# Attention and soft mixture of experts on one core: front and first block scheduled by pairs of tiles, dispatch from a hyperbolic tangent

## The chip, the cores and the metric

One core of one Trainium2 chip runs the whole program. The metric is the device time in microseconds (us) from launch to end, as the median of several runs. The kernel is written in Bass: every engine has its own list of instructions, written out by hand, and the lists meet at semaphores. Short names: PE is TensorE, PEld its weight load, DVE VectorE, ACT ScalarE, POOL GpSimd, SP SyncE (here a queue for DMAs).

## The reference

```python
def ln(x): return (x - mean(x)) / sqrt(var(x) + 1e-5)
# x: (2, 2048, 256); C = 256; N = 64 experts, P = 32 slots each

def attn(x):                       # linear attention, no softmax
    h = ln(x) * norm_w + norm_b
    q, k, v = split(h @ qkv_w.T + qkv_b)
    o = ((q @ k.T) / sqrt(C)) @ v
    return x + o @ proj_w.T + proj_b

def ffn(x):
    logits   = einsum('bmd,dnp->bmnp', x, phi)
    dispatch = softmax(logits, axis=0)            # over the batch, 2 entries
    combine  = softmax(logits over all n*p)       # over 2048 slots
    slots = einsum('bmd,bmnp->bnpd', x, dispatch)
    y     = einsum('bnpd,nde->bnpe', slots, W) + b
    return einsum('bnpd,bmnp->bmd', y, combine)

x = x + ln(attn(ln(x)))
x = x + ln(ffn(ln(x)))
```

## The kernel before, in words

A tile is 128 tokens; each of the two batch entries has 16 (`NJ`). Five stages follow one another.

*Front* (to 51 us). Tiles of x are loaded in groups of four (`load_x`), DVE takes mean and variance (`stats`), POOL works out the scales (`x_terms`), ACT normalises (`xhat`), PE adds each tile to a 256x256 sum and transposes it (`s_tile`, L1184 and L1193). Attention is linear, so it becomes one matrix A for each batch entry: `weight_products` (L1171, L1175) multiplies prepared weights, `T_step`, `R_step`, `A_step` (L1200, L1210, L1220, L1222) combine them with the sum. The prepared weights come from DVE (`bias_columns` L871 to L877, `primed_weights` L891, L894) and from one product on POOL (L430). `phi`, the slot matrix, is split on DVE into two fp16 halves (L927, L929) after a maximum over all partitions on POOL (L437).

*Second norm*. For each pair of tiles PE multiplies with A (`h_pair`, L1234). DVE adds x (`add_x`, L945), ACT squares (`y_squares`, L643), POOL takes the power -1/2 (`y_terms`), DVE adds to the residual (`residual`, L962) and takes statistics (`stats_x2`, L972 and L975), POOL takes the next power (`x3_terms`), ACT writes the normalised x3 (`x3_float`, L652) and its fp16 high half (`x3_hi`), POOL its low half (`x3_lo`, L471). All of it in groups of four tiles, `GROUPS_Y` and `GROUPS_X`.

*Dispatch and slots*. A softmax over two entries is a sigmoid of the difference of logits. POOL subtracts the two batch entries (`xd_diff`, L480), ACT and POOL split the difference (`xd_hi`; `xd_lo`, L487), SP transposes it by DMA (L314) and, for later, x3 (L317). Four blocks of 512 slots follow, each over 16 tiles: PE multiplies the difference with a block of phi (`d_tile`, L1266, six matmuls), ACT takes two sigmoids (`dispatch`, L700) and copies the logit difference, which is stored to DRAM; DVE splits both sigmoids into fp16 halves of 1024 columns (`split`, L952 and L954); PE multiplies tile and dispatch into the slots (`slots`, L1278, twelve matmuls). After a block DVE takes the slots out of PSUM (`slots_out`, L1027). Block 0 is unrolled and interleaved with the second norm, whose late groups it must wait for; blocks 1 to 3 are loops (`block_pe` and so on), in which PE also does the experts of the block before (`y_product`, L1291), with the bias added by DVE (`y_bias`, L1036, L1039). The last group has its `y_product` after block 3, against the loads of expert weights.

*Combine* (from 414 us to the end). For each tile logits again, exp on ACT (L774), transposes by DMA, three products with y (L1351, L1352, L1355), the last norm and the store.

What sets the order is therefore the written list of each engine. This is the part of PE's list in block 0:

```python
for j in range(NJ):
    if j % GJ == 0:
        pe.wait_ge(x3l_ready, 2 * (j // GJ + 1))
    slots(0, j)
    if j + 2 < NJ:
        d_first(j + 2)
    else:
        d_tile(1, j + 2 - NJ)
    if j in (2, 3):
        h_pair(12 + j)
```

## Time and profile before

| what | us |
|---|---|
| median of 3 runs (lowest, highest) | 691.34 (690.93, 692.81) |
| the profiled execution, its own time | 690.47 |
| its span, first to last instruction | 688.7 |
| busy: PE, DVE, ACT, POOL | 618.7, 440.0, 348.2, 246.7 |
| share of the span: PE, DVE, ACT, POOL | 90%, 64%, 51%, 36% |
| PE's mean granted clock, share of 2.4 GHz | 0.97 |

The profile is of one execution. Its span is shorter than its time by what lies around the program. A time of day in the text, as "at 95.72", is counted from the start of the span. A PE row of the timeline gives the stretch from the first start to the last end of its matmuls, and matmuls overlap: the next starts while the last drains.

### The profile page before, as it was taken

How to read it: one execution, taken by the hardware profiler on the slowest of the kernel's cores; microseconds unless marked ns; L12 is line 12 of the kernel's file. 1: busy time of each engine (PE TensorE's matmuls, PEld its weight loads, DVE VectorE, ACT ScalarE, POOL GpSimd, SP SyncE). 2: the span in 40 equal slices, each digit the busy share in tenths (PEclk: the TensorE clock that was granted, in tenths of full speed). 3: DMA queues.
4: the chain of work that ended last, by engine and by line, in shares of the span. 5: the costliest groups of instructions: out<-in, count | busy, mean ns of one | idle time of the engine just before them, and what ended most of it. 6: DMA issues, size and time to landing. Idle time of an engine off the chain costs nothing.

```text
span 688.7 us, 12544 instructions
## 1 busy us (share of the span) xinstructions
PE 618.7 (90%) x3962; PEld 377.5 (55%) x3962; DVE 440.0 (64%) x795; ACT 348.2 (51%) x600; POOL 246.7 (36%) x510
## 2 busy tenths in 40 slices
PE   5899766887999999999999977799999999999992
PEld 4788522333444444444444434367777777777782
DVE  5937666845645555554655568877777777777750
ACT  4565585555433333444443328555566666655550
POOL 5632755954000000000000000166666555666666
PEclk9999969799999999999999999899999999999997
DMA  8900123225133343333334366499999899999991
GB/s 288 393 27 0 31 62 91 63 75 123 61 131 131 130 130 129 127 121 125 127 117 136 118 223 160 118 214 225 213 220 216 198 213 233 225 219 221 214 182 41
DMA packets 190238, 104.52 MB, mean 152 GB/s; under 512 B 152833, under 2 KB 178690, under 8 KB 187906
## 3 DMA queue, kind: packets, MB, share of 16 engines
q1 hardware_dynamic: 183408, 82.07, 48.1%
q10 hardware_dynamic: 6802, 22.09, 9.8%
q8 instruction: 16, 0.26, 0.2%
q14 instruction: 12, 0.10, 0.1%
HBM read 43.32 MB, written 23.07 MB: 96 GB/s over the span
## 4 chain that ended last, share of the span: by engine, by line
PE 66%; DVE 8%; POOL 8%; ACT 7%; issue 5%; DMA 3%; SPq 2%; POOLq 0%; DVEq 0%; ACTq 0%
PE psL L1278 19%; PE psL L1337 10%; PE bk L1266 9%; PE bk L1351 6%; PE bk L1355 6%; PE bk L1352 6%; PE bk L1291 4%; POOL small L395 2%; ACT r_y L652 2%; PE psL L1184 2%; POOL r_xn L471 2%; DMA r_xn<-in_proj_wT 1%; ACT xbuf L643 1%; DVE r L954 1%; ACT r L700 1%
## 5 line engine op out<-in xcount | busy, mean ns | idle before, releaser
L1278 PE MATMUL psL<-r,r_xn 128*128 128x512 f16 x768 | 183.0, 389 | 25.8 <-DVE r L954 25.5
L700 ACT ACTIVATE r<-bk,small 128x512 f32<-128x512 f32 x128 | 80.8, 682 | 140.5 <-PE bk L1266 139.5
L1278 PEld LDWEIGHTS psL<-r,r_xn 128*128 128x128 f16 x768 | 73.9, 100 | 126.8 <-DVE r L954 25.4
L1351 PE MATMUL bk<-r_xn,r 128*128 128x256 f16 x512 | 113.9, 273 | 7.0 <-DMA r<-r 4.0
L1352 PE MATMUL bk<-r_xn,r 128*128 128x256 f16 x512 | 113.8, 273 | 0.0
L952 DVE TENSOR_SCALAR r<-r 128x1024 f16<-128x1024 f32 x64 | 48.5, 758 | 89.8 <-ACT r L700 89.8
L1266 PE MATMUL bk<-phs,xx 128*128 128x512 f16 (+1 forms) x384 | 95.0, 385 | 4.5 <-DMA xx<-r 4.5
L1337 PE MATMUL psL<-phs,xx 128*128 128x512 f16 x384 | 88.3, 387 | 5.7 <-DVE small L1059 4.9
L534 POOL PARTITION_ALL_REDUCE small<-small x1 | 1.2, 1233 | 253.3 <-DVE small L1130 253.3
L774 ACT ACTIVATE r<-psL,small 128x1024 f32<-128x1024 f32 x32 | 38.2, 1198 | 87.7 <-DVE small L1059 87.7
L954 DVE SCALAR_TENSOR_TENSOR r<-r 128x1024 f16<-128x1024 f32 x64 | 80.2, 1253 | 2.2
L1266 PEld LDWEIGHTS bk<-phs,xx 128*128 128x128 f16 x384 | 38.0, 99 | 52.0 <-issue 8.5
L1337 PEld LDWEIGHTS psL<-phs,xx 128*128 (+1 forms) x384 | 37.8, 99 | 51.0 <-issue 11.0
L1355 PE MATMUL bk<-r_xn,r 128*128 128x256 f16 x512 | 61.1, 273 | 0.1
L1351 PEld LDWEIGHTS bk<-r_xn,r 128*128 128x128 f16 x512 | 50.0, 98 | 17.0 <-DVE r_xn L1115 3.7
L587 ACT ACTIVATE r<-bk 128x512 f32<-128x512 f32 (+2 forms) x97 | 50.3, 519 | 16.4 <-PE bk L1355 11.7
L1063 DVE CUSTOM_DVE_ANT_0 r<-psL,xx 128x512 f32<-128x512 f32 x64 | 40.4, 687 | 24.1 <-ACT r L774 24.1
L1352 PEld LDWEIGHTS bk<-r_xn,r 128*128 128x128 f16 x512 | 50.1, 98 | 7.1
L395 POOL TENSOR_TENSOR small<-small,epst 128x1 f32<-128x1 f32 (+2 forms) x58 | 52.0, 897 | 4.8
L1355 PEld LDWEIGHTS bk<-r_xn,r 128*128 128x128 f16 x512 | 50.0, 98 | 6.1 <-DMA r<-xx 0.4
L1075 DVE TENSOR_REDUCE small<-psL 128x1 f32<-128x512 f32 x64 | 41.2, 685 | 11.1 <-PE psL L1337 10.7
L1052 DVE TENSOR_TENSOR xx<-r,xx 128x1024 f16<-128x1024 f32 x32 | 37.9, 1222 | 11.4 <-ACT xx L587 11.4
(117 smaller groups left out, 811.8 us busy)
## 6 DMA issues: line engine op xcount, KB each, us to landing
r<-in_ffn_w SPq DMA_DIRECT2D x16, 1024.0 KB, 6.6
xx<-logit_difference ACTq DMA_DIRECT2D x15, 1024.0 KB, 5.4
logit_difference<-r SPq DMA_DIRECT2D x48, 256.0 KB, 2.4
xres<-in_x SPq DMA_DIRECT2D x8, 512.0 KB, 9.0
logit_difference<-r ACTq DMA_DIRECT2D x16, 256.0 KB, 2.4
out<-r SPq DMA_DIRECT2D x32, 128.0 KB, 2.4
expert_bias<-r ACTq DMA_DIRECT2D x1, 2048.0 KB, 26.3
r<-in_phi SPq DMA_DIRECT2D x1, 2048.0 KB, 18.7
```

The lines of the kernel that those rows point to most:

```text
L395: return nc.gpsimd.tensor_tensor(o, v, epst[:, 0:1].broadcast_to([P, n]), ALU.pow)
L587: return nc.scalar.activation(o, i, ACT.Copy, scale=scale)
L700: ins = nc.scalar.activation(sF[:, j % 2, s, :], bk[j % 2][:, :], ACT.Sigmoid, scale=kap[:, s:s + 1])
L952: own.add(V.tensor_scalar(shl[:, j % 2, 0], sF[:, j % 2], S_SCALE, None, ALU.mult))
L954: V.scalar_tensor_tensor(shl[:, j % 2, 1], sF[:, j % 2], S_SCALE, shl[:, j % 2, 0], ALU.mult, ALU.subtract).then_inc(s_split, 1)
L1075: own.add(V.tensor_reduce(m4[:, kb:kb + 1], psL[:, 512 * kb:512 * kb + 512], AX_X, ALU.max))
L1266: ins = mm(bk[j % 2][:, :], xxT[:, 1, j, hx, k, :], phs[:, hp, k, bass.ds(nb * 512, 512)], start=(k == 0 and hx + hp == 0), stop=(k == K - ...
L1278: ins = mm(psL[:, i * 512:(i + 1) * 512], x3n[:, b, j, hx, k * P:(k + 1) * P], shl[:, j % 2, hs, b, :], start=(j == 0 and hx + hs == 0), s ...
L1337: ins = mm(psL[:, kb * 512:(kb + 1) * 512], xxT[:, 0, bass.ds(j, 1), hx, k, :].rearrange("p j t -> p (j t)"), phs[:, hp, k, kb * 512:(kb + ...
L1351: mm(acc, eT[b][:, 0, t, :], yhl[:, b, t, 0, :], start=(t == 0), stop=False)
L1352: mm(acc, eT[b][:, 0, t, :], yhl[:, b, t, 1, :], start=False, stop=False)
L1355: ins = mm(acc, eT[b][:, 1, t, :], yhl[:, b, t, 0, :], start=False, stop=(t == NT - 1))
```

## The change

- The front loads the first four tiles in two groups. DVE, no longer POOL, multiplies the weights with the norm weight; the centring of the projection goes behind `primed_weights` and has a signal of its own; `weight_products` goes from before tile 14 to after tile 17. The all-reduce of phi goes ahead of the second `residual_terms`.
- The second norm goes by pairs of tiles instead of fours: twice the number of power instructions on POOL, of half the columns.
- The batch difference and its low half go from POOL to DVE.
- The dispatch of entry 0 is (1 + t)/2 and that of entry 1 is (1 - t)/2 with t = tanh(d/2). ACT takes one tanh for two sigmoids, DVE splits 512 columns instead of 1024, and the slots matmuls of both entries read the same t. The constant half of each token sum is put in by `slots_out`, from sums that PE makes once (`token_sums`, `half_sums`) and ACT copies.
- The stores of the logit difference in block 0 go from ACT's queue to SP's, between the transposes.
- The lists of all engines for the second norm and block 0 are written anew; loops and stages behind are otherwise the same.

```diff
-        GROUPS_Y = [0, 1, 4, 5, 2, 6, 3, 7]
-        GROUPS_X = [0, 4, 1, 5, 2, 6, 3, 7]
+        X_GROUPS = [(0, 0, 2), (0, 2, 2)] + [(b, j, GJ) for b in range(B) for j in range(0, NJ, GJ) if b + j]
+        Y_ORDER = [(0, 0), (0, 1), (0, 2), (0, 3), (1, 0), (1, 1), (1, 2), (0, 4), (1, 3), (0, 5), (1, 4), (0, 6), (1, 5), (0, 7), (1, 6), (1, 7)]
+        X_ORDER = [(0, 0), (1, 0), (0, 1), (1, 1), (0, 2), (1, 2), (0, 3), (1, 3), (0, 4), (1, 4), (0, 5), (1, 5), (0, 6), (1, 6), (0, 7), (1, 7)]
...
 # SP
+            def store_d(nb, j):
+                sp.wait_ge(d_copied, nb * NJ + (j + 3))
+                sp.dma_start(d_dram[j, :, bass.ds(nb * 512, 512)], dS[:, j % 2, :]).then_inc(d_stored[j % 2], 16)
+            turn_xd(0); turn_xd(1); store_d(0, 0); store_d(0, 1); turn_xd(2); store_d(0, 2)
+            store_d(0, 3); turn_xd(3); store_d(0, 4); store_d(0, 5); turn_x1(0); turn_xd(4)
...
 # POOL
-                if g == NG - 1:
-                    pool.wait_ge(par_loaded, 16 * N_PAR)
-                    nc.gpsimd.tensor_tensor(w_aug, w_raw, wbc.unsqueeze(1).broadcast_to([P, KS, C]),
-                                            ALU.mult).then_inc(waug_ready, 1)
...
+            residual_terms(0)
             pool.wait_ge(gmax_in, 1)
             nc.gpsimd.partition_all_reduce(gm[:, 0:1], pm[:, 0:1], P, bass.bass_isa.ReduceOp.max).then_inc(gmax_out, 1)
+            residual_terms(1)
...
+            y_terms(0, 0); y_terms(0, 1); x3_terms(0, 0); y_terms(0, 2); x3_lo(0, 0); y_terms(0, 3)
+            y_terms(1, 0); y_terms(1, 1); x3_terms(1, 0); x3_terms(0, 1); x3_terms(1, 1); x3_lo(1, 0)
...
 # ACT
-                for s in range(B):
-                    ins = nc.scalar.activation(sF[:, j % 2, s, :], bk[j % 2][:, :], ACT.Sigmoid, scale=kap[:, s:s + 1])
-                ins.then_inc(s_ready, 1)
+            def tanh(nb, j):
+                act.wait_ge(d_done, nb * NJ + (j + 1))
+                act.wait_ge(s_split, nb * NJ + (j + 1))
+                nc.scalar.activation(tF[:, j % 2, :], bk[j % 2][:, :], ACT.Tanh, scale=khalf).then_inc(t_ready, 1)
+            def d_copy(nb, j):
+                act.wait_ge(d_stored[j % 2], nb * (8 * NJ) + (16 * (j // 2) + 16))
+                copy(dS[:, j % 2, :], bk[j % 2][:, :]).then_inc(d_copied, 1)
+            def token_sums_copy():
+                act.wait_ge(xs_done, 1)
+                for b in range(B):
+                    copy(xsum[:, b], bk[2 + b][:, :]).then_inc(xs_copied, 1)
...
+            xd_hi(7); x3_hi(1, 7); d_copy(0, 12); tanh(0, 13); d_copy(0, 13); token_sums_copy()
+            tanh(0, 14); d_copy(0, 14); tanh(0, 15); d_copy(0, 15); half_sums_copy()
...
 # DVE
+            def weight_scale():
+                dve.wait_ge(par_loaded, 16 * N_PAR)
+                own.add(V.tensor_tensor(w_aug, w_raw, wbc.unsqueeze(1).broadcast_to([P, KS, C]), ALU.mult))
...
             stats(3)
+            stats(4)
             proj_bias()
+            weight_scale()
+            stats(5)
             bias_columns()
-            stats(4)
             primed_weights()
-            stats(5)
+            centre_projection()
             stats(6)
             stats(7)
+            stats(8)
...
-                own.add(V.tensor_scalar(shl[:, j % 2, 0], sF[:, j % 2], S_SCALE, None, ALU.mult))
+                own.add(V.tensor_scalar(thl[:, j % 2, 0], tF[:, j % 2], S_SCALE, None, ALU.mult))
                 own.wait()
-                V.scalar_tensor_tensor(shl[:, j % 2, 1], sF[:, j % 2], S_SCALE, shl[:, j % 2, 0],
+                V.scalar_tensor_tensor(thl[:, j % 2, 1], tF[:, j % 2], S_SCALE, thl[:, j % 2, 0],
                                        ALU.mult, ALU.subtract).then_inc(s_split, 1)
...
+            def xd_diff(p):
+                t2, o2 = slice(2 * p, 2 * p + 2), slice(2 * (p % 2), 2 * (p % 2) + 2)
+                dve.wait_ge(x3_ready, max(X_AT[0, p], X_AT[1, p]) + 1)
+                if p >= 2:
+                    dve.wait_ge(xdl_ready, p - 1)
+                V.tensor_tensor(xd[:, o2], xy[:, 0, t2, :], xy[:, 1, t2, :], ALU.subtract).then_inc(xd_ready, 1)
+            def xd_lo(p):
+                o2 = slice(2 * (p % 2), 2 * (p % 2) + 2)
+                dve.wait_ge(xdh_ready, p + 1)
+                V.tensor_tensor(xdn[:, o2, 1, :], xd[:, o2], xdn[:, o2, 0, :], ALU.subtract).then_inc(xdl_ready, 1)
...
-                                        1.0 / (X_SCALE * S_SCALE), None, ALU.mult).then_inc(slots_evac, 1)
+                                        (0.5 - b) / (X_SCALE * S_SCALE), xhalf[:, i:i + 1],
+                                        ALU.mult, ALU.add).then_inc(slots_evac, 1)
...
 # PE
             for t in range(B * NJ):
-                if t == 14:
-                    weight_products()
                 s_tile(t)
                 if t == NJ + 1:
+                    weight_products()
                     T_step(0)
...
-                                     shl[:, j % 2, hs, b, :], start=(j == 0 and hx + hs == 0), stop=(j == NJ - 1 and hx == 1))
+                                     thl[:, j % 2, hs, :], start=(j == 0 and hx + hs == 0), stop=(j == NJ - 1 and hx == 1))
...
+            def token_sums():
+                pe.wait_ge(y_added, B * NJ)
+                pe.wait_ge(x3l_ready, B * NJ // 2)
+                for b in range(B):
+                    for r in range(NJ // GJ):
+                        for g in range(GJ):
+                            ins = mm(bk[2 + b][g * Q:(g + 1) * Q, :], ones16[:, :],
+                                     x3n[:, b, r * GJ + g].rearrange("p h c -> p (h c)"), start=(r == 0), stop=(r == NJ // GJ - 1))
+                ins.then_inc(xs_done, 1)
+            def half_sums():
+                pe.wait_ge(xs_copied, B)
+                for k in range(K):
+                    for b in range(B):
+                        for h in range(2):
+                            ins = mm(bk[2][:, k * B + b:k * B + b + 1], xsum[:, b, h * C + k * P:h * C + (k + 1) * P], half_mean,
+                                     start=(h == 0), stop=(h == 1))
+                ins.then_inc(xhalf_done, 1)
+            d_first(0); d_first(1); h_pair(0, 7); slots_first(0); d_first(2); slots_first(1)
+            d_first(3); slots_first(2); h_pair(1, 6); d_first(4); slots_first(3); d_first(5)
...
+            d_first(14); token_sums(); slots_first(13); d_first(15); slots_first(14); d_tile(1, 0)
+            half_sums(); slots_first(15); d_tile(1, 1)
```

PE in the front, after the transposes of tile 13; L1184 and L1193 are a tile of the sum, L1171 and L1175 the weight products. Before:

```order
L1193 MATMUL bk<-ident,xbuf 128x128 x2
L1171 MATMUL bk<-r_xn 128x256 x4
L1175 MATMUL bk<-r_xn 128x256 x4
L1184 MATMUL psL<-xbuf 128x256
L1184 MATMUL psL<-xbuf 128x128
```

Now, after tile 17 (L1129 and L1138 are a tile, L1114 and L1120 the weight products, L1145 the T step):

```order
L1138 MATMUL bk<-ident,xbuf 128x128 x2
L1114 MATMUL bk<-r_xn 128x256 x4
L1120 MATMUL bk<-r_xn 128x256 x4
L1145 MATMUL psL<-ident,r_xn 128x128
L1129 MATMUL psL<-xbuf 128x256
L1129 MATMUL psL<-xbuf 128x128
```

The products stand four tiles later, right ahead of the first step that needs them.

DVE at the first splits of block 0. Before, L952 and L954 are the split, L962 the residual, L972 and L975 the statistics, four tiles at once:

```order
L952 TENSOR_SCALAR r<-r 128x1024
L954 SCALAR_TENSOR_TENSOR r<-r 128x1024
L962 SCALAR_TENSOR_TENSOR xres<-r_y,small,xres 128x256 x4
L952 TENSOR_SCALAR r<-r 128x1024
L954 SCALAR_TENSOR_TENSOR r<-r 128x1024
L972 BN_STATS stat<-xres 128x6 x4
L975 BN_AGGR small<-stat 128x2 x4
```

Now, in the third split of the block (L898 and L900 the split, L891 the add of x, L929 the batch difference, L935 its low half):

```order
L891 SCALAR_TENSOR_TENSOR r_y<-xres,small,bk 128x256 x2
L929 TENSOR_TENSOR r<-r_y 128x512
L898 TENSOR_SCALAR r<-r 128x512
L900 SCALAR_TENSOR_TENSOR r<-r 128x512
L935 TENSOR_TENSOR r<-r 128x2x256
L907 SCALAR_TENSOR_TENSOR xres<-r_y,small,xres 128x256 x2
L917 BN_STATS stat<-xres 128x6 x2
L920 BN_AGGR small<-stat 128x2 x2
L898 TENSOR_SCALAR r<-r 128x512
```

Between two splits stand pieces of two tiles, and the difference and its low half stand around a split.

SP's queue after the loads. Before, the loads (L304, L307) and then only the transposes of block 0 (L314 of the difference, L317 of x3):

```order
L304 DMA r<-in_ffn_w 128x8x256 x2
L307 DMA r<-expert_bias 128x256 x2
L314 DMA_TRANSPOSE xx<-r 128x8x128 x2
L317 DMA_TRANSPOSE xx<-r_xn 128x16x128
L314 DMA_TRANSPOSE xx<-r 128x8x128 x2
```

Now (L320 the difference, L326 x3, L331 the stores of the logit difference):

```order
L320 DMA_TRANSPOSE xx<-r 128x8x128 x2
L331 DMA logit_difference<-r 128x512 x2
L320 DMA_TRANSPOSE xx<-r 128x8x128
L331 DMA logit_difference<-r 128x512 x2
L320 DMA_TRANSPOSE xx<-r 128x8x128
L331 DMA logit_difference<-r 128x512 x2
L326 DMA_TRANSPOSE xx<-r_xn 128x16x128
```

Two stores stand between one transposed pair and the next.

## Rows read from the trace of the kernel before

**Rows 1.** Windows by stage: us, then busy time and instructions of PE, PEld, DVE, ACT, POOL; clock, DMA

```profile
9.60:51.46 41.86, 39.21 (x228) 35.18 (x229) 27.59 (x75) 26.61 (x54) 22.94 (x37) 0.96 0.64 228
51.46:84.69 33.23, 28.72 (x133) 24.43 (x132) 22.23 (x58) 19.68 (x58) 16.32 (x22) 0.99 0.07 14
84.69:186.90 102.21, 77.85 (x316) 33.67 (x316) 65.67 (x108) 57.65 (x113) 53.13 (x52) 0.89 0.32 81
186.90:394.40 207.50, 206.10 (x1224) 91.43 (x1224) 111.86 (x129) 82.30 (x141) 0.00 (x0) 1.00 0.38 124
```

**Rows 2.** Groups of PE, 51.46 to 186.9: busy, mean ns | idle before and its releaser

```profile
L1278 PE MATMUL psL<-r,r_xn 128*128 128x512 f16 x192 | 50.6, 420 | 24.3 <-DVE r L954 24.3
L1266 PE MATMUL bk<-phs,xx 128*128 128x512 f16 x108 | 27.9, 399 | 4.5 <-DMA xx<-r 4.5
```

**Rows 3.** Timeline of PE: start us, length us, what, count [idle before, releaser]

```profile
84.69 4.16 PE L1266 MATMUL bk<-phs,xx 128*128 128x512 f16 x12 [4.51 <-DMA xx<-r]
95.72 5.28 PE L1278 MATMUL psL<-r,r_xn 128*128 128x512 f16 x12 [6.86 <-DVE r L954]
...
133.23 5.30 PE L1278 MATMUL psL<-r,r_xn 128*128 128x512 f16 x12 [3.36 <-DVE r L954]
...
163.37 2.76 PE L1278 MATMUL psL<-r,r_xn 128*128 128x512 f16 x12 [1.69 <-DVE r L954]
...
394.45 2.76 PE L1278 MATMUL psL<-r,r_xn 128*128 128x512 f16 x12 [0.95 <-DVE r L954]
...
412.69 1.93 PE L1291 MATMUL bk<-r 128*32 128x256 f32 x32 [2.53 <-DMA r<-in_ffn_w]
```

**Rows 4.** Timeline of PE in the front

```profile
6.69 1.11 PE L1162 MATMUL bk<-ident,bT 128*64 128x128 f32 x4 [6.69 <-DMA bT<-in_ffn_bT]
...
18.11 0.82 PE L1184 MATMUL psL<-xbuf 128*128 128x256 f32 x4
...
22.48 0.82 PE L1184 MATMUL psL<-xbuf 128*128 128x256 f32 x4
...
26.11 3.68 PE L1171 MATMUL bk<-r_xn 128*128 128x256 f32 x8 [2.60 <-DVE r_xn L894]
29.63 1.89 PE L1175 MATMUL bk<-r_xn 128*128 128x256 f32 x8
```

**Rows 5.** Timeline of DVE: first add, and the first split of block 0

```profile
54.25 1.84 DVE L945 SCALAR_TENSOR_TENSOR r_y<-xres,small,bk 128x256 f32<-128x256 f32 x4
...
93.51 0.69 DVE L952 TENSOR_SCALAR r<-r 128x1024 f16<-128x1024 f32 x1 [3.04 <-ACT r L700]
94.24 1.23 DVE L954 SCALAR_TENSOR_TENSOR r<-r 128x1024 f16<-128x1024 f32 x1
```

**Rows 6.** Timeline of POOL in the front

```profile
15.61 3.68 POOL L430 TENSOR_TENSOR r_xn<-r_xn 128x1536 f32<-128x1536 f32 x1 [1.28 <-DMA r_xn<-in_proj_wT]
...
46.16 0.38 POOL L437 PARTITION_ALL_REDUCE small<-small  x1 [5.55 <-issue]
```

**Rows 7.** Groups of the whole program, PE's y product and ACT's dispatch

```profile
L700 ACT ACTIVATE r<-bk,small 128x512 f32<-128x512 f32 x128 | 80.8, 682 | 140.5 <-PE bk L1266 139.5 <-ACT r L587 0.9
...
L1291 PE MATMUL bk<-r 128*32 128x256 f32 x512 | 30.9, 382 | 3.4 <-DMA r<-in_ffn_w 3.4
```

**Rows 8.** Timeline of ACT at the first exp

```profile
408.83 1.28 ACT L774 ACT_TABLE_LOAD   x1 [18.10 <-DVE small L1059]
```

**Rows 9.** Groups of POOL, 51.46 to 186.9

```profile
L487 POOL TENSOR_TENSOR r<-r 128x512 f16<-128x512 f32 x8 | 11.5, 1458 | 2.2 <-ACT r L587 2.2
L480 POOL TENSOR_TENSOR r<-r_y 128x512 f32<-128x512 f32 x8 | 10.2, 1296 | 7.2 <-ACT r_y L652 7.2
```

**Rows 10.** Instructions of line 314, the transposes of the difference on SP

```profile
DMA to landing us min/median/max: 3.1/3.2/4.8
```

**Rows 11.** Groups of DVE, 84 to 187

```profile
L954 DVE SCALAR_TENSOR_TENSOR r<-r 128x1024 f16<-128x1024 f32 x17 | 22.6, 1332 | 0.6
L952 DVE TENSOR_SCALAR r<-r 128x1024 f16<-128x1024 f32 x17 | 16.1, 947 | 31.9 <-ACT r L700 31.9
```

466 lines of the change are left out of this document (179 added, 287 removed).

## The prediction

> **What bounds the kernel now.** I read the windows by stage first, then the groups of TensorE inside the stage with most idle time, then TensorE's own timeline, and last the engines that end its waits. The windows [rows 1] are to be read as length of the stage against PE's busy time. From 186.90 to 394.40 us, blocks 1 to 3, PE is busy 206.10 of 207.50 us at clock 1.00: what only relieves another engine can gain nothing there. The idle time that the change addresses lies ahead of it: 2.7 us in the front (41.86 less 39.21) and 28.9 us from 51.46 to 186.90 (4.51 and 24.36), and in the last of these stretches the granted clock is .89.
>
> Who ends the waits: before the slots matmuls (L1278) PE waits 24.3 us in all for DVE's L954, the second half of the split, and before L1266 4.5 us for the first transposed difference [rows 2]. In the timeline [rows 3] the gaps are 4.51, 6.86 and 3.36 us at 84.69, 95.72 and 133.23. Behind the last two, twelve matmuls take 5.28 and 5.30 us instead of 2.76: PE has fallen from 2.4 to 1.2 GHz, so an idle stretch is paid twice. L954 is only the last link. Groups of four tiles pass through add, square, power, residual, statistics, power, normalise, difference, split in two halves and transpose, and each hop holds back four tiles at once.
>
> **The front.** The weight products stand after tile 13. There PE waits 2.60 us for the DVE chain and then needs 3.68 us for eight matmuls of which the next eight take 1.89 [rows 4]. They now stand after tile 17. A tile costs .874 us (five from 18.11 to 22.48), so PE arrives 3.5 us later than it does now, at 27.0 instead of 23.5. The DVE chain is led now by the product with the norm weight, 1536 columns, which on POOL took 3.68 us [rows 6]; on DVE 1024 columns with two inputs take 1.23 [rows 5], so about 1.9. It was done at 26.1 before; with the centring moved behind it and one statistics group moved ahead I take 25 to 27. So the wait goes: 2.60 us. Without a gap the low clock goes too: 3.68 - 1.89 = 1.79. The first x load is halved, but ACT's first work hangs on the bias rows, for which PE waits until 6.69 [rows 4]; I take 0. The front gives **-4.4 us**, bounds 0 (DVE's chain late by as much as now) and -5. PE begins the h products at 47.1 instead of 51.46.
>
> DVE must by then have split phi. It waits for POOL's all-reduce at 46.16 and adds from 54.25 [rows 5, 6], 8.1 us behind. The all-reduce now goes ahead of the second residual group; with the earlier statistics I put it at 41, and DVE's first add at 49.1, when the first h pair is there. If the all-reduce stayed at 46, PE would run ahead by its banks, but all pairs would come 5 us later: +5 as a bound.
>
> **Block 0.** From 51.46 to 186.92 PE takes 135.5 us. Its own work at full clock: 192 slots and 108 difference matmuls at .216 (twelve end 2.76 after the first starts, .38 of it drain; [rows 3] at 163.37), 64.8 us. 32 h tiles of four fp32 matmuls, also .216 (the 1.89 for eight, [rows 4]), 27.7; the second batch's R and A are eight such matmuls each, 3.5, with a transpose and two bias matmuls 4.2. Sum 96.7. The other 38.8 us are 28.9 idle and 9.9 low clock and drains.
>
> New work on PE: 32 matmuls for the token sums, 512 columns into 32 rows, in turn into four row groups. L1291 has that form in fp32, where 256 columns cost the .216 that 512 cost in fp16: 32 of them take 1.93 us [rows 3], though the mean of one is .382 [rows 7]. So four run side by side and the 32 here cost 1.9 (bound: one after another, 6.9). For sixteen fp32 matmuls of one column there is no row; between .06 each, the pace of L1291, and .216: .9 to 3.5, I take 2.4, nearer to the second, since each brings fp32 weights of 128 columns. **PE's work is then 101.0 us, and without idle time block 0 ends at 47.1 + 101.0 = 148.1.** Blocks 1 to 3 keep their twelve slots matmuls for a tile.
>
> Can the others feed it? Sums of the two windows [rows 1]: DVE 87.9 now; 17 splits lose half of .69 + 1.23 [rows 5] (-16.3); eight differences and eight low halves of 512 columns come in at half of 1.23 (+9.9): 81.5. ACT 77.3, less 17 times one of two sigmoids (.68, [rows 7]): 65.7, and its 16 stores go to SP. POOL 69.4 less 10.2 + 11.5 [rows 9] is 47.7; its terms are twice as many instructions of half the size, and even if all of it doubled it would be 95. None reaches 101; DVE is the fullest. What remains is the loop from pair to pair: difference 1.3, tanh .7, split .96, low half .6, transpose .4 to start and 3.2 to land [rows 10], next difference. With five hand-overs of .1 that is 7.7, and PE takes 2 x 3.9 = 7.8 for two tiles: no slack. The order gives it some later (the low half stands two or three tiles ahead). But DVE's splits average 1.33 and .95 in this stretch against the 1.23 and .69 of the single rows [rows 11, 5]. I add 1 to 1.3 us for each of seven pairs: **8 us of idle time**. Bounds: 0, and 24.3, what PE waits for L954 now. In it is SP: difference tiles' stores now stand between the transposes, so that a transpose can wait for a copy that ACT has yet to make.
>
> Block 0 ends at 148.1 + 8 = 156.1 instead of 186.9: **-30.8**, of which the 4.4 of the front are a part.
>
> **Behind it.** Blocks 1 to 3: 0, hidden by PE's 206 us; without that cover the halved splits would gain, not lose. At 394.45 PE waits .95 for L954 behind a bias add [rows 3]; half of that split goes, so **-0.9**. Of the table loads the one before exp (1.28 at 408.83, [rows 8]) goes if tanh and exp need none between them. It is hidden: at 412.69 PE waits for expert weights [rows 3], not for exp. 0.
>
> Sum -30.8 - .9 = **-31.7**. The profiled execution took 690.47 (span 688.7), .87 below the median of the runs, 691.34: 658.8 by its clock, **659.6** as median.
>
> **Rivals.**
> 1. *PE never waits.* For it: every other sum is below PE's. Against: the loop without slack. 691.34 - 38.8 - .9 = 651.6. Chance 0.13.
> 2. *DVE and POOL hold each other up.* The differences leave POOL for DVE, and each has two SBUF inputs. The splits' two halves take 2.28 us here instead of 1.92 [rows 11, 5], a fifth on top. If the rest of DVE's 81.5 grow alike, to 97, DVE is as full as PE and no split is early: 1.3 us late at each of 16 tiles makes 21 us of waits instead of 8: 659.6 + 13 = 673. 0.13. The Trainium skill, "SBUF — State Buffer", section "Who interferes with whom", says that a VectorE instruction with two SBUF inputs and a GpSimd instruction that reads SBUF shut each other out for a whole instruction. The long splits agree with it; by that rule what moves from GpSimd to VectorE doesn't end the contention, it leaves fewer large GpSimd instructions to contend with.
> 3. *The clock stays low (slower).* Place: difference and slots matmuls of block 0. PE would idle a little before each tile instead of much before each fourth, and restart at 1.2 GHz each time, as behind the gap at 95.72. Price: 300 matmuls at .43 instead of .216, +64.8 on 659.6: 724. It makes the kernel slower once 31.7/64.8 = 49% of them run low. Against: behind the gaps PE is back at 2.76 for a group one tile later. 0.03.
> 4. *The change does not do what it says*: pairs in a fixed order wait on each other as fours did and block 0 keeps its length. Only front and .9 count: 686. 0.03.
>
> **Numbers.** Forecast (3 to 15 us of idle time in block 0) 0.68; the rivals 0.13, 0.13, 0.03, 0.03. Range 650.5 to 673: it takes in rival 1, rival 2 up to its value, and the bounds of the token sums (+5), of the front (+4.4) and of DVE's start (+5). About 0.3% (2 us) is what a measurement of this kernel can tell from no change. Faster 0.96, same 0.01, slower 0.03.
>
> **What would show it.** Right: the weight products run without a wait, eight in 1.9; h products from 47; first difference tile near 74 instead of 84.69; no gap over 2 us before a slots group; clock at 1.00 up to block 1, whose slots begin near 156; 501 us from there to the end. Wrong: a gap of PE at the token sums or half sums (it would wait for ACT's copies), transposes landing after more than 5 us, or PE busy for more than 101 us between the h products and block 1.

## The result and the profile after

The changed kernel takes **660.06 us** (median of 4 runs, 658.74 to 666.30) against 691.35 for the kernel before in the same measurement (690.93 to 692.81): a ratio of 0.956, 95% interval 0.951 to 0.961. Forecast were 659.6 us and a range of 650.5 to 673. The profiled execution took 660.40 us with a span of 658.4. The total is right to .5 us; the terms are less so, and several errors cancel. Of all executions behind this document one is left out, of the run called "first group of four" below, which took 1086.52 us at a granted clock of .56.

| us | before | forecast | after |
|---|---|---|---|
| PE's first h product | 51.46 | 47.1 | 48.76 |
| DVE's first add | 54.25 | 49.1 | 53.88 |
| first difference tile on PE | 84.69 | near 74 | 77.47 |
| slots of block 1 begin | 186.92 | 156.1 | 159.83 |
| from there to block 3's last slots group | 207.53 | 206.6 | 205.26 |
| from there to the last y product | 18.24 | as before | 17.27 |
| from there to the end of the span | 276.0 | as before | 276.0 |

The windows of the profile after, at the bounds that the forecast gave the stages, a little ahead of the measured ones (columns as in [rows 1]):

```profile
9.60:47.00 37.40, 36.43 (x215) 32.90 (x216) 26.36 (x78) 26.61 (x53) 15.04 (x32) 1.00 0.72 260
47.00:76.00 29.00, 27.88 (x133) 23.79 (x132) 21.75 (x50) 15.86 (x45) 18.70 (x34) 1.00 0.02 5
76.00:156.50 80.50, 73.08 (x363) 34.80 (x362) 58.15 (x128) 51.62 (x119) 50.27 (x83) 1.00 0.44 104
156.50:364.00 207.50, 207.50 (x1238) 93.75 (x1236) 76.07 (x131) 56.27 (x96) 0.00 (x0) 1.00 0.38 124
```

The stretch from the first difference tile to block 1 has lost 24.36 - 7.42 = 17 us of idle time (between its measured bounds, 77.47 and 159.83, 7.10 are left), and the granted clock is 1.00 in it instead of .89. The timeline of PE after, the rows with the waits that answer to [rows 3], the new work, and the two places behind the blocks:

```profile
57.06 1.99 PE L1165 MATMUL psL<-r_xn 128*128 128x256 f32 x8 [1.12 <-ACT r_xn L554]
77.47 2.75 PE L1202 MATMUL bk<-phs,xx 128*128 128x512 f16 x12 [0.32 <-DMA xx<-r]
100.68 2.75 PE L1214 MATMUL psL<-r,r_xn 128*128 128x512 f16 x12 [1.34 <-DVE r L900]
109.52 2.75 PE L1214 MATMUL psL<-r,r_xn 128*128 128x512 f16 x12 [0.91 <-DVE r L900]
118.59 1.46 PE L1202 MATMUL bk<-phs,xx 128*128 128x512 f16 x6 [0.94 <-ACT r L554]
131.13 2.75 PE L1214 MATMUL psL<-r,r_xn 128*128 128x512 f16 x12 [1.48 <-DVE r L900]
143.22 1.47 PE L1202 MATMUL bk<-phs,xx 128*128 128x512 f16 x6 [0.84 <-DMA xx<-r]
144.62 1.91 PE L1252 MATMUL bk<-r_xn,ones 128*32 128x512 f16 x32
154.25 1.84 PE L1262 MATMUL bk<-small,xbuf 128*128 128x1 f32 x16
365.09 2.76 PE L1214 MATMUL psL<-r,r_xn 128*128 128x512 f16 x12 [0.15 <-DVE r L900]
382.36 1.93 PE L1227 MATMUL bk<-r 128*32 128x256 f32 x32 [1.70 <-DMA r<-in_ffn_w]
```

From the first h product on no gap is longer than 1.48 us up to block 1, and no group of twelve takes more than 2.76: PE never falls to 1.2 GHz in block 0. For the experiments one row says most: the window from PE's first h product to its first slots of block 1, "block 0" from here on. For the changed kernel it is:

```profile
48.76:159.83 111.07, 102.52 (x497) 58.40 (x496) 80.36 (x181) 67.91 (x163) 68.97 (x117) 1.00 0.33 79
```

PE is busy 102.52 us and idle 8.55 (forecast: 101.0 and 8). More than 101 us of work in this stretch was one of the forecast's signs of being wrong, the only one that came; its cause is below. For the kernel before the same window, 51.46 to 186.92, has 106.58 busy and 28.9 idle.

### The profile page after: what moved, and what is told of

Read it like the earlier page. It is cut to its first block, busy times and chain, and to the rows that moved or that the text cites. A ratio compares the mean times of both kernels' runs of the same rounds, so it can differ in the third digit from the quotient of the medians.

```text
span 658.4 us, 12694 instructions
## 1 busy us (share of the span) xinstructions
PE 613.0 (93%) x4010; PEld 378.4 (57%) x4010; DVE 396.6 (60%) x813; ACT 310.7 (47%) x545; POOL 239.4 (36%) x555
## 4 chain that ended last, share of the span: by engine, by line
PE 67%; POOL 9%; DVE 8%; issue 7%; DMA 5%; ACT 3%; SPq 1%; POOLq 0%; DVEq 0%; ACTq 0%
PE psL L1214 20%; PE psL L1296 11%; PE bk L1202 10%; PE bk L1310 7%; PE bk L1311 7%; PE bk L1314 7%; PE bk L1227 4%; POOL small L415 4%; DMA r_xn<-in_proj_wT 1%; DMA r<-r 1%; DVE xres L907 1%; DMA xx<-r 1%; POOL r_xn L486 1%; DVE r_xn L1058 1%; DMA r<-in_ffn_w 1%
## 5 line engine op out<-in xcount | busy, mean ns | idle before, releaser
L1214 PE MATMUL psL<-r,r_xn 128*128 128x512 f16 x768 | 176.3, 379 | 4.7 <-DVE r L900 4.7
L639 ACT ACTIVATE r<-bk,small 128x512 f32<-128x512 f32 x64 | 43.8, 685 | 151.8 <-PE bk L1202 150.7
L1202 PE MATMUL bk<-phs,xx 128*128 128x512 f16 (+1 forms) x384 | 93.2, 379 | 2.8 <-DMA xx<-r 1.9
L898 DVE TENSOR_SCALAR r<-r 128x512 f16<-128x512 f32 x64 | 28.1, 439 | 88.9 <-ACT r L639 88.9
L415 POOL TENSOR_TENSOR small<-small,epst 128x2 f32<-128x2 f32 (+3 forms) x75 | 57.5, 767 | 6.2
L1018 DVE TENSOR_REDUCE small<-psL 128x1 f32<-128x512 f32 x64 | 41.2, 686 | 10.6 <-PE psL L1296 10.3
L900 DVE SCALAR_TENSOR_TENSOR r<-r 128x512 f16<-128x512 f32 x64 | 44.3, 693 | 2.2
```

The lines of the kernel that those rows point to most:

```text
L415: return nc.gpsimd.tensor_tensor(o, v, epst[:, 0:1].broadcast_to([P, n]), ALU.pow)
L639: nc.scalar.activation(tF[:, j % 2, :], bk[j % 2][:, :], ACT.Tanh, scale=khalf).then_inc(t_ready, 1)
L900: V.scalar_tensor_tensor(thl[:, j % 2, 1], tF[:, j % 2], S_SCALE, thl[:, j % 2, 0], ALU.mult, ALU.subtract).then_inc(s_split, 1)
L1018: own.add(V.tensor_reduce(m4[:, kb:kb + 1], psL[:, 512 * kb:512 * kb + 512], AX_X, ALU.max))
L1202: ins = mm(bk[j % 2][:, :], xxT[:, 1, j, hx, k, :], phs[:, hp, k, bass.ds(nb * 512, 512)], start=(k == 0 and hx + hp == 0), stop=(k == K - ...
L1214: ins = mm(psL[:, i * 512:(i + 1) * 512], x3n[:, b, j, hx, k * P:(k + 1) * P], thl[:, j % 2, hs, :], start=(j == 0 and hx + hs == 0), stop ...
```

## Experiments

The runs came in four groups, and in each the kernel before was run too: 690.85, 691.82, 690.33 and 690.05 us. Each ratio is to that. Times of different groups are compared below as they stand, so differences of 1 to 2 us between them are not told apart.

| run | us | ratio, 95% interval | block 0 | PE idle in it |
|---|---|---|---|---|
| the changed kernel | 660.06 | 0.951 to 0.961 | 111.07 | 8.55 |
| pairs, two sigmoids | 674.06 | 0.974 to 0.978 | 121.95 | 19.48 |
| fours, tanh | 683.33 | 0.988 to 0.993 | 129.49 | 19.28 |
| differences on POOL | 675.33 | 0.977 to 0.982 | 126.67 | 21.70 |
| adds by batch | 658.73 | 0.952 to 0.956 | 110.87 | 8.79 |
| weight products at 14 | 662.93 | 0.955 to 0.960 | 115.36 | 9.56 |
| no sums | 657.31 | 0.948 to 0.953 | 107.19 | 8.32 |
| stores on ACT | 665.81 | 0.959 to 0.966 | 114.05 | 10.08 |
| first group of four | 660.05 | 0.953 to 0.958 | 110.83 | 8.24 |
| POOL also adds | 674.97 | 0.974 to 0.980 | 125.29 | 19.35 |
| POOL also fills | 670.44 | 0.968 to 0.973 | 121.55 | 16.97 |
| lists shifted | 659.38 | 0.951 to 0.956 | 108.61 | 6.74 |
| lists again | 658.57 | 0.953 to 0.955 | 107.70 | 5.82 |

### Pairs without tanh, tanh without pairs

The first undoes the tanh in the changed kernel (dispatch, splits, token sums):

```diff
-                nc.scalar.activation(tF[:, j % 2, :], bk[j % 2][:, :], ACT.Tanh, scale=khalf).then_inc(t_ready, 1)
+                for s in range(B):
+                    ins = nc.scalar.activation(sF[:, j % 2, s, :], bk[j % 2][:, :], ACT.Sigmoid, scale=kap[:, s:s + 1])
+                ins.then_inc(t_ready, 1)
...
-            d_first(14); token_sums(); slots_first(13)
+            d_first(14); slots_first(13)
```

> The changed kernel with its new lists, but with two sigmoids and splits of 1024 columns as before; token sums and half sums, no longer needed, are left out. Theory A (order by pairs carries the gain, the tanh only gives the loop its slack): the loop of a pair grows by half a split, .96 us, and one activation, .6 us, so 1.6 us x 8 pairs = +13, less 3.5 us of sums: 668 to 672 us. Theory B (the tanh carries the gain, since DVE and ACT lose 16 and 11 us of work): most of the 31 us comes back, 683 us or more. Blocks 1 to 3 get back 1.5 to 2.3 us under both.

The second puts the same tanh, splits and sums into the kernel before and leaves its order of fours:

```diff
+                if j == 12:
+                    token_sums()
+                if j == 14:
+                    half_sums()
```

> The kernel before with its groups of four and its old lists, but with one tanh, splits of 512 columns, token sums and half sums. Theory A: the nine waits before slots stay, each shorter by some .96 + .6 us where split or sigmoid ended it, about -10 in block 0 and -2 in blocks 1 to 3, plus 3.5 of sums: 681 to 687 us. Theory B: 670 us or less.

Measured: 674.06 and 683.33. The first is 2 us above the range of its theory A and far below theory B, the second is inside theory A. The first run has all other edits too (front, differences on DVE, stores on SP); the second has tanh and sums alone. Against 690.85 pairs alone bring 16.8 us and tanh alone 7.5, 24.3 in all; together they bring 31.3 (691.35 - 660.06), 7 more than the sum. By the profiled executions, against 690.47, it is 5. PE's timelines say where from, first of the pairs without tanh, then of the fours with it:

```profile
108.14 4.08 PE L1213 MATMUL psL<-r,r_xn 128*128 128x512 f16 x12 [2.80 <-DVE r L902]
...
144.40 4.44 PE L1213 MATMUL psL<-r,r_xn 128*128 128x512 f16 x12 [3.73 <-DVE r L902]
```

```profile
84.06 5.28 PE L1290 MATMUL bk<-phs,xx 128*128 128x512 f16 x12 [5.00 <-DMA xx<-r]
92.41 4.44 PE L1302 MATMUL psL<-r,r_xn 128*128 128x512 f16 x12 [3.08 <-DVE r L975]
113.23 4.40 PE L1302 MATMUL psL<-r,r_xn 128*128 128x512 f16 x12 [4.24 <-DVE r L975]
138.61 5.30 PE L1302 MATMUL psL<-r,r_xn 128*128 128x512 f16 x12 [3.99 <-DVE r L975]
```

In each alone PE still idles 19 us in block 0, against 28.9 before and 8.55 with both, and some of its gaps are still long enough that the groups behind them take 4.08 to 5.30 us instead of 2.75. PE's loss beyond its own work (96.7 us, with the sums 100.4) was 38.8; it is 25.3 with pairs, 29.0 with tanh, 10.6 with both. Idle time nearly adds up: 9.4 and 9.6 us less alone, 20.3 together. The rest of the loss, low clock and drains, doesn't: 9.9 us before, 5.8 with pairs, 9.8 with tanh, 2.1 with both. So neither part is spare, and most of what goes beyond the sum in block 0 is the clock, which comes back with the last long gaps. What tanh saves here is not ACT's time alone: with two sigmoids DVE's splits are 1024 columns wide again, 35.7 us in 17 tiles against 20.0.

### Does PE feel the sums? Does it feel DVE's late start?

Without token sums and half sums (the edit takes the two calls, ACT's two copies and one wait, and fills the halves with zeros):

> The changed kernel without token sums, half sums and ACT's copies of them; the halves are zero, so the output lacks the constant half of the slots. Theory A: PE is the bound at that place and the sums cost their 1.91 + 1.84 us and the waits around them: 656 to 656.5. Theory B: they fill time in which PE would wait for the loop of pairs anyway: 658 to 660.

Measured 657.31, between the ranges of the two theories, and by the intervals not told apart from the changed kernel. The profile decides: block 0 is 107.19 us long instead of 111.07, 3.9 less, as much as the 3.75 that the matmuls take, and the wait ahead of them at the difference tile stays (.83). That is theory A's mechanism: PE is the bound at the end of block 0, and what it is given there shows in the time.

At its start it is not so. POOL and DVE of the changed kernel, around the all-reduce, POOL first:

```profile
41.91 0.38 POOL L451 PARTITION_ALL_REDUCE small<-small  x1 [5.46 <-issue]
49.42 0.80 POOL L439 TENSOR_SCALAR small<-small 128x16 f32<-128x16 f32 x1 [7.12 <-issue]
```

```profile
53.88 1.66 DVE L891 SCALAR_TENSOR_TENSOR r_y<-xres,small,bk 128x256 f32<-128x256 f32 x4 [3.73 <-POOL small L444]
```

The all-reduce is done at 42.3 (forecast: 41), and phi's split follows. But DVE's first add waits for the second residual group of POOL, which I had not put into the chain: behind the all-reduce POOL does nothing for 7.12 us, and the group ends at 53.84. The edit lets the first adds and squares wait for the terms of their own batch entry alone:

```diff
                 if i == 0:
-                    dve.wait_ge(r0_ready, 2)
+                    dve.wait_ge(r0_ready, 1)
+                if i == Y_AT[1, 0]:
+                    dve.wait_ge(r0_ready, 2)
```

> The changed kernel, but DVE's first add and ACT's first square wait for the first batch's residual terms only; the second batch's are waited for at that batch's first pair. In the changed kernel DVE waits 3.73 us (to 53.88) for the second batch's terms, which POOL starts 7.1 us after the all-reduce. Theory A (the chain of pairs sets the pace from its start): first add at 50.2, PE's wait of 1.12 us before the R step goes and the later waits shrink: -2 to -4, 656 to 658 us. Rival (the loop in the middle of block 0 sets the pace, the start has slack): only the 1.12 us, 659 us.

Measured 658.73, 1.3 us less, which the two intervals don't tell apart; by the profile the first difference tile comes at 75.64 instead of 77.47, but block 0 begins .42 earlier for other reasons and its length is 110.87 instead of 111.07. The rival is the nearer: DVE's first add starts at 50.33, the 1.12 us at 57.06 go, and what comes earlier runs into later waits for transposes (1.61 at 112.04 instead of .72, 2.09 at 142.60 instead of .84). Against PE's first h product DVE starts 3.1 us earlier than in the changed kernel, and block 0 is .2 us shorter, so the forecast's bound of +5 was far too dear.

### The front

Weight products before tile 14 again:

```diff
             for t in range(B * NJ):
+                if t == 14:
+                    weight_products()
                 s_tile(t)
                 if t == NJ + 1:
-                    weight_products()
                     T_step(0)
```

> The changed kernel with the weight products before tile 14 again (ACT's copy of them one place earlier too). Theory A (the sum of the prediction): PE waits for DVE's chain and then runs the products slowly, 2.60 + 1.79 = 4.4 us more than the 660.1 of the changed kernel, so 664. Theory B: DVE's chain is shorter now (the scaling is on DVE, one statistics group is moved), so the wait is only in part there: 661 to 663. Theory C: the start of block 0 is set by DVE and POOL, not by PE, and a front that is some us longer on PE costs nothing: 660.

Measured 662.93: 2.9 us above the changed kernel and not told apart from it by the intervals. The profile shows what the median hides. PE and DVE of this run:

```profile
25.66 1.99 PE L1114 MATMUL bk<-r_xn 128*128 128x256 f32 x8 [0.26 <-DVE r_xn L840]
...
59.01 2.77 PE L1165 MATMUL psL<-r_xn 128*128 128x256 f32 x8 [2.51 <-ACT r_xn L554]
```

```profile
18.07 1.76 DVE L815 TENSOR_TENSOR r_xn<-r_xn 128x1536 f32<-128x1536 f32 x1 [4.60 <-DMA r_xn<-in_proj_wT]
```

In the old place the products wait .26 us, not 2.60, and run at full speed. So the new place was not needed for that: it is the list of DVE that takes the wait away. How, the rows of DVE show, before and then in this run (L871 and L809 are the bias columns, L873 and L819 the start of the centring, L894 and L840 the end of the chain):

```profile
15.91 3.66 DVE L871 CUSTOM_DVE_ANT_0 r<-r_xn 128x256 f32<-128x256 f32 x1
...
20.88 0.67 DVE L873 TENSOR_REDUCE small<-r_xn 128x2 f32<-128x512 f32 x1
...
25.89 0.17 DVE L894 TENSOR_TENSOR r_xn<-small 128x6 f32<-128x6 f32 x1
```

```profile
23.18 0.42 DVE L809 CUSTOM_DVE_ANT_0 r<-r_xn 128x256 f32<-128x256 f32 x1
...
25.43 0.17 DVE L840 TENSOR_TENSOR r_xn<-small 128x6 f32<-128x6 f32 x1
25.51 0.68 DVE L819 TENSOR_REDUCE small<-r_xn 128x2 f32<-128x512 f32 x1
```

From the landing of the weights to the end of the chain it is 10.5 us before (from 15.56) and 7.5 in this run (from 18.07). Of these 3.0 us some 1.6 are the product: beside POOL's, from 15.61 to 19.29 [rows 6], one instruction of DVE's bias columns took 3.66 us, where .42 is usual, and DVE's own product costs only 1.68. The other 1.4 are the centring, which now stands behind the chain. The product itself ended no earlier in this run (19.75) than on POOL before (19.29). No run tests product and centring one by one.

The .26 are owed to weights that landed 1.8 us later than in the changed kernel's profiled execution (L815 starts at 16.31 there), with which the all-reduce and DVE's first add came 2 us later too (43.87 and 55.82). PE waited 2.51 us at 59.01 and then ran at a mean granted clock of .84 up to 80 us, which makes block 0's work 105.80 us instead of 102.52. The edit touches no load. Theory A falls, and the time is in theory B's range; what the edit alone costs the profile doesn't show beyond the .26, and the medians can't tell.

PE's wait of 2.60 is not a fixed price of the old front either. The run with tanh alone keeps that front. In its profiled execution the bias rows landed at 8.51 instead of 6.69, PE reached the weight products at 26.77, just behind DVE's chain (26.32), and did not wait; its h products began at 50.33, 1.1 us earlier than in the kernel before.

First x group whole again:

```diff
-        X_GROUPS = [(0, 0, 2), (0, 2, 2)] + [(b, j, GJ) for b in range(B) for j in range(0, NJ, GJ) if b + j]
+        X_GROUPS = [(b, j, GJ) for b in range(B) for j in range(0, NJ, GJ)]
```

> The changed kernel with its first four tiles of x in one load group again (statistics one group fewer, in the old places). Theory A: the .44 us by which the first matmul is later (bias rows land at 7.13 instead of 6.69) and the longer low clock come from the one DMA more ahead: 659.3 or less. Theory B: the halves bring ACT's first tile earlier and this is worth as much or more: 660 to 662.

Measured 660.05; span 657.9 against 658.4. The first matmul came at 9.77 instead of 10.09, the h products at 48.46 instead of 48.76, and nothing of it was left. "I take 0" for the halved load fits; neither theory is supported.

### Stores of the difference on ACT's queue

```diff
+            def act_store(j):
+                act.wait_ge(d_copied, j + 3)
+                act.dma_start(d_dram[j, :, 0:512], dS[:, j % 2, :]).then_inc(d_stored[j % 2], 16)
...
-            turn_xd(0); turn_xd(1); store_d(0, 0); store_d(0, 1); turn_xd(2); store_d(0, 2)
+            turn_xd(0); turn_xd(1); turn_xd(2)
```

> The changed kernel with the stores of block 0's logit difference issued by ACT, each right behind its copy, instead of SP. SP then has only transposes. Theory A: a transposed pair is held back on SP by stores that wait for ACT's copies; without them first blocks of 1 to 2 us of PE's waits go: 657 to 659. Theory B: the issue costs ACT as much as SP gives, and the waits move: 659.5 to 662.

Measured 665.81, 5 us slower by the medians (661.9 to 668.7; the intervals just touch; the profiled execution took 663.42, so the profile shows only half of the loss): both theories miss. Block 0 is 3.0 us longer. The queue of SP and, then, PE:

```profile
100.92 1.23 SPq L320 DMA_TRANSPOSE xx<-r  x1
102.20 4.11 SPq L326 DMA_TRANSPOSE xx<-r_xn  x1
110.01 1.23 SPq L320 DMA_TRANSPOSE xx<-r  x1
```

```profile
106.98 2.35 PE L1207 MATMUL bk<-phs,xx 128*128 128x512 f16 x6 [2.12 <-DMA xx<-r]
109.12 3.60 PE L1219 MATMUL psL<-r,r_xn 128*128 128x512 f16 x12
```

Freed of the stores, SP issues the big transpose of x3 right behind the pair of 100.92; in the changed kernel two stores stand between the two, and it comes at 107.14, 7.7 us behind its pair. The pair lands after 6.0 us, where the slowest of the changed kernel takes 4.0, and PE waits 2.12 us for it, behind which the next groups run slowly (2.35 and 3.60). So the fear in the prediction, that stores between the transposes hold them back, did not come true: in this kernel PE waits less with the stores there. That the x3 transpose is what makes the pair late is argued from its place in the queue; the runs with new lists below move it, together with other things. What takes the other 2 us is open.

### Who holds back the loop of pairs: POOL's work or its reads?

The differences and their low halves go back to POOL, everything else stays:

```diff
-                V.tensor_tensor(xd[:, o2], xy[:, 0, t2, :], xy[:, 1, t2, :], ALU.subtract).then_inc(xd_ready, 1)
+                nc.gpsimd.tensor_tensor(xd[:, o2], xy[:, 0, t2, :], xy[:, 1, t2, :], ALU.subtract).then_inc(xd_ready, 1)
```

> The changed kernel with batch difference and its low half back on POOL, by pairs. Theory A: DVE loses 10 us and POOL gains 18 to 22 in a stage of 111, so that POOL becomes the fullest (some 92): +2 to +8, 662 to 668 us. Rival (VectorE and GpSimd shut each other out, so that the large instructions on POOL are what hurts): 670 us or more, with DVE's splits and residuals longer in the trace. Rival (where they stand doesn't matter): 660 us within 2.

Measured 675.33: half of the gain is gone, with POOL busy 85.92 of 126.67 us, far from full. That is in the range of the expectation's contention rival, and its second sign is there too. The second half of DVE's split, from 76 to 160 us, first here, then in the changed kernel:

```profile
L915 DVE SCALAR_TENSOR_TENSOR r<-r 128x512 f16<-128x512 f32 x14 | 15.0, 1071 | 0.5
```

```profile
L900 DVE SCALAR_TENSOR_TENSOR r<-r 128x512 f16<-128x512 f32 x17 | 11.8, 693 | 0.6
```

But POOL is also busy 17 us more from 76 to 160 us (67.24 for 50.27), and this run does not say which of the two costs the time, hence a pair of runs: useless work of some 20 us on POOL, reading in one and filling in the other.

```diff
+                for r in range(2):
+                    own.wait()
+                    own.add(nc.gpsimd.tensor_tensor(scr[:, :], scr[:, :], scr[:, :], ALU.add))
```

```diff
+                for r in range(4):
+                    own.wait()
+                    own.add(nc.gpsimd.memset(scr[:, :], 0.0))
```

> The changed kernel with work on POOL that nobody needs: behind each of the 16 low halves of x3 two additions of 256 columns, whose operands are read from SBUF (some 1.3 us for each low half, estimated from the 1.15 us of the 512 columns of the low half itself; 20 us in all). Its twin has the same place and about the same time on POOL, but fills memory and reads nothing. Theory A (DVE and POOL hold each other up, rival 2): this one costs more than its twin by some of the 15 us that the differences cost on POOL: 670 to 680 here against 662 to 670 for the twin. Theory B (POOL is simply full, and the pairs wait for its terms): both cost the same, 668 to 678.

> The twin: behind each low half four fills of 256 columns, which read nothing. Theory A (contention through reading): 662 to 670, less than the one that reads. Theory B (POOL's fullness): 668 to 678, the same as the one that reads.

Measured 674.97 and 670.44: +14.9 and +10.4 over the changed kernel. The first lies in the ranges of both theories, the second in theory B's and just above theory A's; that the two differ, by 4.5, is theory A's sign. POOL's groups from 76 to 160 us and DVE's split and low half in the same window, first with additions, then with fills (columns as in [rows 2]):

```profile
L492 POOL TENSOR_TENSOR scr<-scr 128x256 f32<-128x256 f32 x30 | 23.1, 771 | 1.2
...
L905 DVE SCALAR_TENSOR_TENSOR r<-r 128x512 f16<-128x512 f32 x14 | 11.2, 797 | 0.5
L940 DVE TENSOR_TENSOR r<-r 128x512 f16<-128x512 f32 x7 | 6.3, 902 | 1.4 <-ACT r L559 1.2
```

```profile
L492 POOL MEMSET scr<- 128x256 f32 x60 | 19.6, 327 | 2.6
...
L905 DVE SCALAR_TENSOR_TENSOR r<-r 128x512 f16<-128x512 f32 x15 | 10.4, 693 | 0.5
L940 DVE TENSOR_TENSOR r<-r 128x512 f16<-128x512 f32 x8 | 5.8, 731 | 1.5 <-ACT r L559 1.4
```

Fills leave DVE's split at the 693 ns of the changed kernel; additions make it 797, and the low half 902 instead of 731. So the contention is real, and of 15 us the larger part, 10, comes without it: POOL's terms and low halves are part of what a pair waits for, and about half of each us added there is waited for, though POOL is idle a third of the time. The rest, 4.5 us by the medians, is contention and the 3.5 us by which the additions turned out longer than the fills; the two aren't separated further. How the 15 us of the differences on POOL divide is not shown by this pair: there the split's second half is at 1071 ns, here at 797.

One place of the changed kernel shows the contention in single instructions, DVE's and POOL's timelines:

```profile
117.66 0.87 DVE L907 SCALAR_TENSOR_TENSOR xres<-r_y,small,xres 128x256 f32<-128x256 f32 x2
...
120.68 2.68 DVE L907 SCALAR_TENSOR_TENSOR xres<-r_y,small,xres 128x256 f32<-128x256 f32 x2
```

```profile
120.56 2.51 POOL L486 TENSOR_TENSOR r_xn<-r_y,r_xn 128x512 f16<-128x512 f32 x2
```

The same two residual instructions take .87 us where POOL has only its small terms and 2.68 while it works out two low halves: each is held for about the length of one POOL instruction. The Trainium skill, "SBUF — State Buffer", section "Who interferes with whom", says that a VectorE instruction with two SBUF inputs and a GpSimd instruction that reads SBUF shut each other out for a whole instruction; these rows agree with it.

### Other lists

From the run with adds by batch: transposes of x3 behind those of the difference on SP, squares and power terms of a pair ahead of the normalising of the pair before, tanh ahead of the halves. For one pair, in ACT's list:

```diff
-            tanh(0, 3); x3_float(0, 3); y_squares(1, 4); x3_float(1, 3); d_copy(0, 3); tanh(0, 4)
-            xd_hi(3); y_squares(0, 6); d_copy(0, 4); x3_hi(0, 3); tanh(0, 5); x3_hi(1, 3)
+            tanh(0, 3); x3_float(0, 3); y_squares(1, 4); d_copy(0, 3); tanh(0, 4); y_squares(0, 6); x3_float(1, 3)
+            x3_hi(0, 3); x3_hi(1, 3); xd_hi(3); d_copy(0, 4); y_squares(1, 5); tanh(0, 5); d_copy(0, 5)
```

> The changed kernel, with the first adds waiting for their own batch's terms (as in the earlier run: 658.7), the transposes of x3 behind those of the difference on SP, and from tile 4 on the lists of ACT, DVE and POOL moved so that squares and power terms of a pair stand ahead of the normalising of the pair before, and a tanh ahead of the halves. Theory A: of the 8.9 us in which PE waits in block 0 of that run about half is order, which this takes away: 653 to 656. Theory B: DVE, ACT and POOL each have 9 us of work for a pair of tiles against PE's 7.8 to 9.5, so the waits only move: 657 to 660.

Measured 659.38 (656.04 to 659.52; the profiled execution is the fastest of them): the range of theory B, though PE's idle time in block 0 went from 8.79 to 6.74 by the profile. One wait of 2.71 us stood out, at 137.14 for the split of tile 12, so that split and its tanh went ahead of the last difference:

> The run before this with one piece in another order: ACT's tanh of tile 12 and DVE's split of it stand ahead of the last normalising and the last difference. In its profile PE waited 2.71 us at 137.14 for that split, of 6.6 us in all. Theory A: some 2 us of them go and the transpose of the last pair is late by at most .8: 1 to 2 us less than the 659.4 of the run before, 657 to 658.5. Theory B: the wait moves whole to the difference tile of the last pair: 659 to 660.

Measured 658.57 (657.68 to 658.82), just above theory A's range and below theory B's. By the profile block 0 is down to 107.70 us with 5.82 idle, 3.4 us shorter than in the changed kernel; PE's timelines, first of the first list, then of the second:

```profile
137.14 2.75 PE L1217 MATMUL psL<-r,r_xn 128*128 128x512 f16 x12 [2.71 <-DVE r L903]
```

```profile
139.83 1.47 PE L1205 MATMUL bk<-phs,xx 128*128 128x512 f16 x6 [1.85 <-DMA xx<-r]
...
416.74 0.28 PE L1313 MATMUL bk<-r_xn,r 128*128 128x256 f16 x1 [1.96 <-DMA r<-r]
```

The 2.71 became 1.85 for the last transposed pair. Of the 3.4 us the median keeps 1.5, less than the intervals can tell: the last y product of the profiled execution is 3.2 us earlier, and the combine stage, which no edit touched, is 1.0 us longer (277.0 from there to the end instead of 276.0), with waits for its own loads. Both kernels with new lists beat the one before; that they beat the changed one is not shown.

## Why the prediction was right, and where its terms were off

*What bounds the kernel* held: blocks 1 to 3 stayed at PE's pace, 27 of 30 us of the gain lie before them, and no clock was lost in block 0. Rival 3 (low clock at each small gap) is out: behind gaps of up to 1.48 us a group of twelve takes 2.75.

*The front*: -2.7 instead of -4.4. The products run without a wait at 28.69 in 1.89 us, as forecast. The first matmul starts .44 later, because the bias rows land at 7.13 instead of 6.69, the low clock of the first tiles costs .70 more, and there is a wait of .48 at 27.54. I had put the cause in two places, DVE's shorter chain and the later place, and by the run with the old place the first is enough. The chain got shorter by its order and by an instruction that POOL's product no longer holds up, which the prediction did not see. And the run with tanh alone reached its h products at 50.33 with the old front, so of the 2.7 us 1.1 lie within what landing times do.

*DVE's start*: forecast 49.1, measured 53.88. The step that failed is "DVE must by then have split phi": it named one of two things that the first add waits for. The second residual group was moved behind the all-reduce, and I never asked what waits for the instruction that is moved back. It cost a wait of 1.12 us and .2 of block 0's length, not 5: PE's list has the second batch's steps and free banks between (argued from the list).

*Block 0*: from first h product to block 1 109.0 forecast, 111.07 measured. Idle 8.55 against 8. Work 102.5 against 101.0: the token sums were right (1.91), the half sums .56 cheaper (1.84 for 2.4), and some 2 us were missing. Ten gaps, before each of which the drain of the last matmul (.38 less .216) is counted as busy, make 1.6 of them; the prediction has that drain beside the group of 2.76 us, and I left it out of the sum. POOL's work was put at 47.7 us and is 68.97: a power instruction for a pair takes .79 us where one for four tiles took 1.28, so twice the number costs 25.3 us instead of 20.5, and the small instructions around it grow from 8.9 to 20.2 us. The bound of 95 covered it. DVE's sum was right (80.36 for 81.5).

*The loop from pair to pair* was the right object only in part. The 8.55 us of idle time fit the 8 that its lack of slack was to cost, but the loop as summed has no work of POOL in it, and its first term, 1.3 for the difference, is POOL's price, where DVE takes .81. The runs show that POOL's work is waited for, about .5 us for each us more (10.4 for 19.6), and that order alone takes the idle time from 8.79 to 5.82. So the size of this term came right partly by luck.

*Rival 2* (DVE and POOL hold each other up) did not come true for this change: DVE is busy 80.36 us, not 97. With the differences on POOL the time is 675, and its price of 21 us of waits is what that run showed (21.70); how much of it is contention and how much POOL's longer work is open.

*Behind block 0*: -3.2 instead of -.9. The wait of .95 is .15 now, as forecast (-.8). Blocks 1 to 3 were given 0 and lost a further 1.5: from one y product to the next the kernel before took 17.97, 17.54, 17.60, 17.74, 17.74, 17.54, 17.60 and 17.82 us in the first two of these blocks and 17.51 after them, the changed kernel 17.50 to 17.52 throughout. These excesses make 1.5 us; one of them is listed as a wait for the second half of the split (.28 at 201.00), the rest are too small to be listed. With "busy 206.10 of 207.50" I had called the stage full. Of the 1.4 us left .9 were the wait that I counted by itself, at 394.45; the other .5 were such small waits, and the rest of the 1.5 is drain ahead of them, counted as busy (206.09 before, 205.11 now). 1.0 lies between the last slots and the last y product, most of it expert weights that landed sooner in this execution (PE's last wait for them 1.70 instead of 2.53, [rows 3]), which I would not credit to the change. The table load before exp is gone, and the combine stage is as long as before (276.0).

So -31.7 was forecast and -30.3 came by the spans of the profiled executions (-30.1 by their times): front 1.7 short, block 0 2.1 short, behind it 2.3 better. That the median fell to within .5 us of 659.6 is in part luck.

## To carry to other kernels

When several engines pass work round a loop, look for the engine whose us are waited for, not for the one that is full: POOL was idle a third of the time, and 20 us of useless work on it cost 10. When an engine's wait disappears, look in the rows before and after for what got shorter: in the front the place of the products had been credited, and the wait went without it. When an instruction is moved back, list who waits for it, and when it is moved forward, what it is put in front of. Two edits that each remove part of a long gap can together be worth more than their sum, because here the clock, too, came back only with the last long gaps.

## What the runs showed of the hardware beyond what was expected

- POOL does nothing for 5.46 us ahead of the all-reduce over partitions and for 7.12 us behind it (5.68 and 7.50 in the run with the weight products at 14), with nothing to wait for in the profile; the all-reduce itself takes .38.
- Sixteen matmuls of one fp32 column take 1.84 us, .115 each. Their loads of fp32 weights (192 ns each, overlapping) stretch over 1.97 us, as long as the matmuls; that the loads set the pace is not tested.
- A residual instruction of DVE took .44 us beside small terms on POOL and 1.34 next to POOL's low halves. Over block 0 its mean is 671 ns in the changed kernel, 660 with 20.9 us of fills more on POOL and 736 with 24.6 us of additions more.
- Beside POOL's product with the norm weight (3.68 us, 15.61 to 19.29 before) one instruction of DVE's bias columns took 3.66 us instead of .42.
- Behind gaps of 2.71 and 2.72 us (the first new list at 137.14, the additions on POOL at 143.15) PE's group ran at full speed, 2.75; behind 2.12 and 2.76 (stores on ACT, differences on POOL) it ran slowly, 2.35 for six and 4.44 for twelve. In the kernel before a group ran at full speed behind 3.23 us at 147.12, and at half speed behind 3.36 at 133.23. The length of a gap alone doesn't tell whether the clock falls.
- With the same loads, DVE's product with the norm weight, which waits for the weights to land, starts between 15.75 and 16.99 us in ten profiled executions and at 18.07 in one, whose all-reduce and first add came later with it.
